# All sixteen query pairs of a cross-attention computed ahead of it, and three smaller reorderings

## The reference

```python
x = x + memory_attention(layernorm(x))                 # 8 memory heads of 128
x = x + cross_attention(layernorm(x), ctx)
x = x + router_ffn(layernorm(x))                       # 64 experts, the 8 best kept

def cross_attention(latents, context):                 # per batch item: 64 query rows, 128 keys
    hidden = concatenate([context, latents], axis=1)
    q = (latents @ Wq).reshape(b, 64, 4, 8, 128)       # 4 key heads, 8 query heads to each
    k = (hidden @ Wk).reshape(b, 128, 4, 128)
    v = (hidden @ Wv).reshape(b, 128, 4, 128)
    attn = softmax(einsum('bqhgd,bkhd->bhgqk', q, k) * 128 ** -0.5)
    out = einsum('bhgqk,bkhd->bqhgd', attn, v)
    return out.reshape(b, 64, 4096) @ Wo
```

## Time and profile before

| | |
|---|---|
| median of 3 runs | 699.23 us (699.2 to 699.68) |
| the profiled execution, its own time | 699.29 us |
| its span, first to last instruction | 697.5 us |
| busy | PE 687.2, PEld 579.3, DVE 520.5, ACT 351.1, POOL 133.8 us |
| mean granted clock of TensorE | 0.996 of full speed |

### The profile page before, as it was taken

The page is one execution under the profiler, slowest core; times in us unless marked ns, Lnnn a source line. Parts: engine busy times, 40 slices in busy tenths (PEclk is TensorE's granted clock), DMA queues, the critical chain, the costliest instruction groups (busy, mean ns, idle before and its releaser), DMA issues.

```text
span 697.5 us, 11041 instructions
## 1 busy us (share of the span) xinstructions
PE 687.2 (99%) x3560; PEld 579.3 (83%) x3560; DVE 520.5 (75%) x1098; ACT 351.1 (50%) x1047; POOL 133.8 (19%) x136
## 2 busy tenths in 40 slices
PE   8999999999999999999999999999999999999996
PEld 7888888888878788888888888888888888788884
DVE  3774966778877888677678876767877657878887
ACT  4454845455443454454346643555635435755543
POOL 0296000000512232022020220210202000322321
PEclk9999999999999999999999999999999999999998
DMA  9996240001325557433342733423643414231101
GB/s 329 371 351 245 67 145 1 1 0 46 121 76 193 184 160 251 142 122 106 107 152 68 233 105 105 150 84 103 191 143 113 141 41 129 77 115 61 46 32 60
DMA packets 70605, 90.14 MB, mean 129 GB/s; under 512 B 4192, under 2 KB 48480, under 8 KB 70560
## 3 DMA queue, kind: packets, MB, share of 16 engines
q1 hardware_dynamic: 65632, 81.71, 35.7%
q10 hardware_dynamic: 4928, 7.87, 3.1%
HBM read 62.29 MB, written 27.26 MB: 128 GB/s over the span
## 4 chain that ended last, share of the span: by engine, by line
PE 93%; DVE 3%; ACT 2%; POOL 1%; issue 1%; ACTq 0%; DVEq 0%; POOLq 0%
PE bank L978 24%; PE bank L907 23%; PE bank L727 13%; PE bank L1091 8%; PE bank L881 6%; PE bank L1147 6%; PE bank L1121 4%; PE bank L718 2%; PE bank L1047 1%; PE bank L846 1%; PE bank L768 1%; PE bank L812 1%; DVE forms L1566 1%; PE bank L802 1%; PE bank L750 0%
## 5 line engine op out<-in xcount | busy, mean ns | idle before, releaser
L978 PE MATMUL bank<-regA,oT 128*128 128x512 f32 x762 | 180.2, 391 | 0.2 <-DVE oT L1566 0.2
L978 PEld LDWEIGHTS bank<-regA,oT 128*128 128x128 f32 x762 | 142.0, 188 | 29.6 <-DVE oT L1566 0.4
L1474 ACT ACTIVATE probs<-bank,negmax 128x128 f32<-128x128 f32 x256 | 89.9, 377 | 42.8 <-DVE negmax L2007 42.8
L907 PE MATMUL bank<-xnT,forms 128*128 128x512 f32 x432 | 108.8, 396 | 0.5 <-DVE qbuf L1776 0.4
L907 PEld LDWEIGHTS bank<-xnT,forms 128*128 128x128 f32 x432 | 79.0, 188 | 17.6 <-DVE qbuf L1776 1.9
L907 PE MATMUL bank<-regC,forms 128*128 128x512 f32 x324 | 83.8, 397 | 1.6 <-DVE qbuf L1776 0.9
L1181 ACT CAST oT<-bank 128x512 fp32r<-128x512 f32 (+1 forms) x66 | 37.7, 573 | 79.5 <-PE bank L1147 76.5
L907 PEld LDWEIGHTS bank<-regC,forms 128*128 128x128 f32 x324 | 59.0, 188 | 13.4 <-DVE regC L1566 1.3
L1181 ACT CAST pT<-bank 128x512 fp32r<-128x512 f32 x64 | 34.6, 593 | 66.9 <-PE bank L1121 66.7
L727 PE MATMUL bank<-regC,xnT 128*128 128x512 f32 x256 | 68.0, 396 | 0.0
L648 POOL TENSOR_TENSOR diff<-wq_raw 128x256 f32<-128x256 f32 x17 | 13.4, 786 | 283.3 <-DVE forms L1566 283.3
(11 more groups left out here) (195 smaller groups left out, 1058.8 us busy)
## 6 DMA issues: line engine op xcount, KB each, us to landing
q_dram<-qbuf SPq DMA_DIRECT2D x32, 512.0 KB, 3.2
qbuf<-q_dram SPq DMA_DIRECT2D x31, 512.0 KB, 4.8
raw<-in_L_xattn_Wo SPq DMA_DIRECT2D x4, 2048.0 KB, 10.5
wq_raw<-in_L_xattn_Wq SPq DMA_DIRECT2D x16, 512.0 KB, 4.1
raw<-in_L_attn_Wo SPq DMA_DIRECT2D x6, 1024.0 KB, 8.9
k_ring<-keys_dram SPq DMA_DIRECT2D x32, 128.0 KB, 3.5
v_raw<-vals_dram SPq DMA_DIRECT2D x64, 64.0 KB, 3.4
resid<-in_x SPq DMA_DIRECT2D x4, 512.0 KB, 11.6
```

Of the source, the lines that this page charges most:

```text
L907: last = nc.tensor.matmul(k_bank[:, :], forms[:, p[1], a, i, c, :], right(b)[:, c, :], start=j == 0, stop=j == 5)
L978: last = nc.tensor.matmul(bank[7][:, :], oT[:, a, h, :], wo[:, b, h, :], start=h == 0 and i == 0, stop=h == GH - 1 and i == 2)
L1474: last = nc.scalar.activation(probs[:, bb, p, :], bank[bb][:, p * P:(p + 1) * P], ACT.Exp, bias=negmax[:, bb, p:p + 1], accum_out=rowsum[: ...
```

## The change

- PE, ACT, DVE and SP run all 18 pairs in one loop ahead of the attention. Pairs 6 to 17 (the title's "ten between" counts otherwise; by the code it is twelve, of the first of which two products already stood ahead) leave the steps. The steps of all groups are then alike, divided where the rule above says so.
- In the pair loop, DVE does the low half of S2 (`inner_low`) after sum 21 instead of before sum u3.
- At the entry to the pairs ("key stage"), the last value product of the latents goes to bank 0 instead of bank 3, its save on ACT comes after two of the four input sums' high halves, and sum 11 of pair 0 comes before its u2.
- POOL makes the low halves of Wo of heads 3 to 7 for groups 1 and 2 as well, and of heads 3 to 5 for group 3, where DVE takes heads 6 and 7 one step later.
- Start: two dummy transposes fewer, and one transposition one product earlier. End: 12 dummy transposes on PE before the last expert's weights; the last row's negated maximum by one instruction; the copy of the last normalised rows ahead of the scaling of the rows before.

```diff
@@ SP
-            for p in range(LEAD):
-                load_pair(p + 2)
+            for p in range(PAIRS):
+                if p + 2 < PAIRS:
+                    load_pair(p + 2)
...
-                    store_pair(0, p - KPAIRS, p)
+                    store_pair((p - KPAIRS) // 4, (p - KPAIRS) % 4, p)
...
-            sp.wait_ge(q_stored[0], 16 * LEAD)
+            for f in range(2):
+                sp.wait_ge(q_stored[f], 16 * PAIRS)
@@ POOL
-            for h in range(4, GH):
-                pool.wait_ge(wo_hi, GH * (KV - 1) + h + 1)
...
+            for g in range(1, KV):
+                for h in range(3, GH - 2 if g == KV - 1 else GH):
+                    pool.wait_ge(wo_hi, GH * g + h + 1)
...
@@ PE
-            for p in range(LEAD + 1):
+            for p in range(PAIRS):
                 pair = (p, p % 2)
                 product_1(pair)
...
@@ PE, step
-                if pair and t % 2:
-                    product_1(pair)
-                    product_6(pair)
-                elif pair:
-                    product_4(pair)
...
+            spin(12)
             expert_weights(NT - 1)
@@ DVE, pairs
+            for p in range(PAIRS):
+                later = p + 1 < PAIRS
+                if p and later:
                     direct_low(p + 1, (p + 1) % 2)
...
+                if p and later:
+                    outer_low(p + 1, (p + 1) % 2)
+                sum_u3(p)
+                sum_21(p)
+                if later:
+                    inner_low(p + 1, (p + 1) % 2)
+                sum_22(p)
+                sum_u4(p)
...
@@ DVE, step
-                if p is not None:
-                    if t % 2:
-                        sum_11(p)
-                        sum_u3(p)
-                    else:
-                        sum_22(p)
-                        sum_u4(p)
-                        sum_12(p)
```

More of the change, by code:

```diff
@@ L934, in product_4 @@
             def product_4(p):
-                pe.wait_ge(q_summed, 7 * p[0] + 2)
+                pe.wait_ge(q_summed, 7 * p[0] + 2 if follows(p[0], 1) else 1)
                 pair_product(p, Z, A22, lambda b: t_block(T4, b))
             def product_5(p):
+                if not follows(p[0], 1):
+                    pe.wait_ge(q_summed, 2)
                 pair_product(p, Y, S1, lambda b: t_block(T1, b))
@@ L1127, in step @@
                     expert_mix(t - 3)
[L1128 to L1131, removed]
-                    product_5(pair)
-                    product_3(pair)
-                elif divided:
+                if divided and not first_step:
                     if t == 0:
@@ L1378, in t_high @@
                 high(t_block((T2, 3, T4, T1)[r], 0), sums[:, (1, 2, 3, 0)[r], :, :]).then_inc(t_hi, 1)
-            for t in range(NT):
+            for t in range(NT - 1):
                 save_latent_values(t)
@@ L1465, in step @@
                 n = 8 * g + t
-                pair = pair_of(g, t) if has_pair(g, t) else None
-                slot = (LEAD + (t + 1) // 2 + 1) % 2
                 for bb in range(2):
@@ L1477, in step @@
                     last.then_inc(exp_done, 1)
-                if t % 2 and pair is not None:
-                    copy_1(pair)
                 if not (last_group and t == 7):
@@ L1484, in step @@
                     v_high(g, t + 1)
-                if first_step or t % 2 and has_pair(g, t + 2):
-                    summed_high(pair + 1, slot)
                 if t == 0 and not first_step:
                     act.wait_ge(wo_loaded, 16 * g + 16)
-                    for h in range(4 if pair is not None else 2):
+                    for h in range(2):
                         act.wait_ge(wo_used, (GH - 1) * (g - 1) + h + 1)
@@ L1502, in step @@
                     high(pT[:, bb, 0, :], bank[bb][:, :]).then_inc(pT_hi, 1)
-                if t == 0 and not first_step and pair is None:
+                if t == 0 and not first_step:
                     act.wait_ge(proj_done, 8 * g)
@@ L1522, in step @@
                 if t == 0 and not first_step:
-                    if pair is not None:
-                        act.wait_ge(proj_done, 8 * g)
-                    for h in range(4 if pair is not None else 5, GH):
+                    for h in range(5, GH):
                         wo_high(g, h)
-                if t % 2 == 0 and has_pair(g, t + 3):
-                    direct_high(pair + 2, (slot + 1) % 2)
                 if last_group and 2 <= t < NT - 1:
@@ L1797, in sum_11 @@
                     dve.wait_ge(q_stored[0], 16 * p)
-                if follows(p, KPAIRS + 1) and not follows(p, LEAD + 1):
+                if follows(p, KPAIRS + 1) and not follows(p, OWN + 1):
                     dve.wait_ge(q_kept, p - KPAIRS)
@@ L2015, in step @@
                     expert_rows(t - 2)
-                p = pair_of(g, t) if has_pair(g, t) else None
-                slot = (LEAD + (t + 1) // 2 + 1) % 2
-                if first_step:
-                    sum_11(p)
-                if t % 2 and has_pair(g, t + 2):
-                    direct_low(p + 1, slot)
                 for bb in range(2):
@@ L2050, in step @@
                     low(pT[:, bb, 1, :], bank[bb][:, :], pT[:, bb, 0, :]).then_inc(pT_lo, 1)
-                if p is None:
+                if not first_step:
                     add_projection(n, t)
                 if t == 0 and not first_step:
-                    for h in range(2, 4):
-                        wo_low(g, h)
+                    wo_low(g, 2)
                 if last_group and t == 2:
@@ L2074, in step @@
                             oT[:, 0, heads, cols]).then_inc(oT_lo, 1)
-                if t == 0 and not first_step and p is not None:
-                    for h in range(4, GH):
-                        wo_low(g, h)
                 if last_group and t == NT - 1:
```

147 lines of the change are left out of this document (64 added, 83 removed).

## The result

| | before | after |
|---|---|---|
| median | 699.35 us (699.2 to 699.68, 6 runs) | 720.43 us (719.54 to 721.87, 6 runs) |
| the profiled execution, its own time | 699.29 us | 719.75 us |
| its span | 697.5 us | 717.3 us |
| mean granted clock of TensorE | 0.996 | 0.996 |

The changed kernel takes 1.0302 times as long, 95% interval 1.0291 to 1.0312: 3.0% slower, where 2.2% were forecast. The time of 720.43 lies inside the range of 702 to 723.

What follows compares the result with a forecast made beforehand. PE, busy 99% of the span, bounds the kernel, but the weight-buffer loop would pace the moved pairs. Pairs +121.7, steps -104.7, end -1.2 sum to +15.8 on 699.29: 715 us, 2.2% slower, range 702 to 723.

Steps and rivals of the forecast that it cites:

- the loop around the one buffer: Pairs ahead of attention: each weight load waits for the previous pair's S2 low half; 9.89 a period against PE's 9.53.
- Entry to the pairs: Product 1 to product 3 of pair 0: waits mostly removed, product 3 at 198.8 with the start's 0.3, instead of 201.29.
- The turn: One round of the pair loop after the change: bounds 9.9 and 11.2, middle 10.5 taken, for 14 turns.
- the row of 4.4 behind the 5.1: Weight load at 263.40, store at 263.82, landed after 4.4 instead of 3.6; hence 5.1 from issue to `direct_low`.
- Contention: Pair loop: DVE's S1 low half beside POOL's last sum, up to 0.48 more a turn.
- Where PE waits: Pair loop: PE waits 0.5 to 1.2 a turn before product 3 or 4, for DVE's `qbuf`.
- First step: First attention step without its 30 pair matmuls: 4.23 to the last exponential plus a 4.3 tail, 8.5; bounds 7.5 and 11.
- Contention is at its upper bound: Rival: turns of 11.1, 8.4 more, or the clock falls in the first step, some 3; 718 to 723; chance 20%.
- The next 22 steps and the boundaries: Steps after the first: 22 at 9.49, 208.8, plus 2.8 for groups 1 and 2 getting group 3's boundary loss.
- The end: Last part: clock kept up by dummy transposes 0.4, copy and DVE instruction 0.6; with group 3's boundary -1.2.
- The rival of PE-paced pairs: Pair loop: PE paces turns at 9.55 through sooner loads or shorter DVE path, 13.3 less, 702; chance 15%.
- The rival on the other side: Pair loop and group boundaries: DVE's queue shorter than read, turns at 9.55 and boundaries costing 0; 698; chance 7%.

Runs made afterwards that it cites:

- e9: The changed kernel with ACT's copy of product 1 ahead of the cast of the next weights instead of behind it: 720.62 us, ratio 1.0305.
- e6: e2 with SP loading the first steps' k and q early in the pair loop, before the last stores: 704.58 us, ratio 1.0076.
- e2: The changed kernel with a second weight buffer for the odd pairs, so a load is issued a turn earlier: 704.47 us, ratio 1.0067.
- e8: e6 with products 4, 5 and 3 of the last pair back inside the first attention step: 700.53 us, ratio 1.0015.
- e5: e2 with POOL making the low halves of Wo of groups 1 and 2 on only 8 of 512 columns: 703.24 us, ratio 1.0055.
- e1: The changed kernel with DVE's low half of S2 put back ahead of sum u3 in the pair loop: 708.79 us, ratio 1.0134.
- e3: The changed kernel with the first store of a query pair waiting for sum u4 instead of sum 21: 718.03 us, ratio 1.0277.

## Why the prediction was right

The sign, the main mechanism (the loop around the one buffer) and its place were right, and the time was 5.4 us too low. In the first step something happened that it had only as a rival, and in the turn two errors of opposite sign happened to cancel. Of the 5.4, 4.0 are the span (717.3 against 713.3), 0.66 lies around the span (2.45 instead of the 1.79 of before), and 0.7 is the profiled execution against the median. The span's part by the terms of the sum:

- **Entry to the pairs.** Product 3 of pair 0 was put at 198.8 and started at 198.75.
- **The turn.** This is the largest miss by sum and the smallest by piece: 10.61 instead of 10.5, 14 times, +1.5; the two turns ahead of them 19.8 instead of 19.4, the last piece 11.0 instead of 10.9. Inside the turn shown, the way from issue to `direct_low` was put at 5.1 and took 5.11; from there S1's low half, u3, 21 and S2's were put at 2.9, 3.50, 4.28 and 4.88 and started at 2.90, 3.57, 4.35 and 4.97. So the term for POOL's contention, taken at half of 0.48, was about 0.07 on the path. What made up for it was the landing: the row of 4.4 behind the 5.1 was near the rule and not the dear case, with 3.8 to 4.5 and a median of 4.2 over the loads. Too much for contention and too little for landing gave 10.5 together, near 10.6; that is luck.
- **Contention.** In the turn shown S1's half took 0.74 instead of 0.69, while POOL's last sum beside it, at 291.33, took 1.07 instead of 0.73. The dearer part fell on POOL, whose last sum was not on the path. In rows 7 it was the other way round: POOL's sum began first (246.52) and took 0.73, DVE's began at 246.64 and took 0.90 instead of 0.42. In the turn shown DVE began first (291.05) and POOL at 291.33. In these rows the loss falls mainly on the one that began second, and the prediction put it all on DVE. The Trainium skill (GPSIMD Engine Reference, section Specifications) says that GpSimd's SBUF interfaces are shared with VectorE, with contention where a DVE instruction has two SBUF inputs. The trace agrees with the contention, but not with the prediction's reading that VectorE loses the whole overlap, by which the turn would have been dearer.
- **Where PE waits.** Product 3 (0.54, of its weight load) and product 4 (0.22) were named; product 7, for the copy behind the late cast on ACT, was not. By e9 this costs nothing.
- **First step.** Put at 8.5, took 9.45, +0.95. The term that was too small is the tail of 4.3 behind the start of the last exponential, which took 5.22 (382.34 to 387.56). DVE's multiply for the second half starts at 383.08 and the transposes at 383.82, and the next scores stand 3.74 behind these. That stretch ran at the clock's lower level. The four transposes took 1.07 instead of 0.66, and the last three value products, which begin at 386.30, when DVE's second half is there, took 1.26 instead of 0.68. That is 1.0 in all, an estimate from these rows, and so about the whole miss. The prediction had the clock falling here, for "some 3", in the rival *Contention is at its upper bound* and not in its sum; this half of that rival came true at a third of its price. What it gave as the reason for an upper bound of the step, the load of q behind the last store, is not it (e6).
- **The next 22 steps and the boundaries.** Put at 211.6, took 599.55 - 387.56 = 211.99. The steps around the start of group 1 take 9.77 + 10.49 = 20.26, by the prediction 20.4. Group 2's boundary reaches over four steps (9.77, 10.41, 9.87, 9.63) and costs 1.7. That groups 1 and 2 would get group 3's loss of 1.4, from nothing, was the right reading. One step of group 2 waited 0.19 more for q.
- **The end.** Put at -1.2 with group 3's boundary, measured -0.5. The clock did rise, as the windows show (columns as above), against 0.52 in the last 5.30 us of the kernel before:

```profile
709.00:712.00 3.00, 2.70 (x21) 2.43 (x21) 2.58 (x11) 1.66 (x5) 0.55 (x1) 1.00 0.23 87
712.00:717.30 5.30, 1.51 (x10) 0.88 (x7) 2.66 (x11) 1.08 (x2) 0.00 (x0) 0.78 0.28 99
```

  From the last scores to the end it is 717.3 - 688.59 = 28.71, before 697.5 - 668.14 = 29.36: 0.65 less, where 1.0 was forecast. The chain of the last 4 us, which before went through PE's last products (693.42, 0.81), now goes through ACT's scaling of the rows (713.30, 0.82) and DVE (714.15, 0.48), so that a still faster PE would be off the path. Group 3's boundary did not get shorter by 0.2 but longer by 0.2: its four steps take 44.75 instead of 44.56, since the one at 629.33 takes 12.69 instead of 12.38; PE waits there 0.20 for a small load, the experts' bias. No run took these apart.

The rival of PE-paced pairs (702) is what e2 shows at 704.5: PE does pace them once a load has slack, but one buffer does not give it. The rival on the other side needed empty boundaries too, and even with every pair at 9.52 the time is above before.

Where the cover went can be added up from the starts of PE's rows in the two profiled executions. The first step of the kernel before ends here:

```profile
265.55 1.95 PE L1091 MATMUL bank<-k_ring,qbuf 128*128 128x128 f32 x16
```

| | before | after | pair matmuls that came or went, at 5.44 / 24 each | after - before - those |
|---|---|---|---|---|
| start to product 3 of pair 0 | 201.29 | 198.75 | | -2.5 |
| from there to the first scores | 53.15 | 179.36 | 492 more, 111.5 | +14.7 |
| the first step | 11.11 | 9.45 | 30 fewer, -6.8 | +5.1 |
| the 22 steps behind it | 313.72 | 211.99 | 462 fewer, -104.7 | +3.0 |
| from step 23 to the end | 118.23 | 117.75 | | -0.5 |

The last column adds up to the +19.8 of the span. The loop is the largest part, then the unfilled first step, then the boundaries of groups 1 and 2, and the smaller edits give 3.0 back. The experiments agree with it as far as they go. e2 took back 16.0, the loop's 14.7 and the 1.4 that pairs 1 to 5 already lost before. e8 took back 4.05 of the first step's 5.1, with 18 of the 30 matmuls back in it. e5 took back 1.2 of the boundaries' 3.

## What to carry to other kernels

Before moving work to a place where nothing else runs, write down the period of its slowest loop, transfers and all four engines included, beside the period of TensorE: work that was hidden between other steps for 28 us a turn needs 10.6 when it stands alone, and one more buffer was worth more there (16.0) than the better order on DVE (11.6). A wait of the bounding engine is not yet a price: take it away (e9) and see whether the loop's period moves. The same reordering on DVE was worth -1.9 with slack in the load and +11.6 without, so an order is to be judged together with the buffers around it. And where a step loses the work that filled TensorE's waits, look at the granted clock of that step too: the waits of 2.37 and 0.74 were followed by some 3.4 us at 0.50.

## What the runs showed of the hardware

- The landing of a 512 KB load differs with what is issued next to it (medians): 3.7 with a store 1.39 behind (e1), 3.8 with the store after u4, 1.19 behind in the turn shown (e3), 4.2 with a store 0.42 behind (after), 4.6 to 4.7 in the kernel with two buffers, where the load mostly goes out right behind a store.
- DVE and POOL side by side do not slow each other alike. With DVE 0.28 ahead, its 128x512 subtraction took 0.74 instead of 0.69 and POOL's 128x256 took 1.07 instead of 0.73 (after). With POOL 0.12 ahead, POOL's took 0.73 and DVE's 128x256 took 0.90 instead of 0.42 (before).
- The granted clock fell from 1.00 to 0.50 in the first step of every profiled kernel with all pairs ahead but e8, for 3 to 7 us, after PE had waited 2.37 and 0.74 us. With the 18 matmuls in that step (e8, waits of DVE 0.58), and in the kernels with the pairs between the steps, it stayed at 1.00.
- The granted clock stayed at full speed in the stretch 709 to 712, where PE was busy 2.70 of 3.00 us, with the 12 dummy transposes among it; in the stretch 690 to 693 before, with 1.15 in 3.00, it stood at 0.89.
